# Attention with two versions, swapped: which version an engine jumps over, a group of rows loaded earlier, and a sign set first

## The reference

```python
x = x + xattn(ctx_1024, layernorm(x), mask, ...)      # keys and values: 77 rows of context and the 1024 tokens themselves
x = x + ffn(layernorm(x), ...)                        # a shared expert, and 8 routed ones of which each token takes 2

# xattn, per batch
q = ln @ Wq;  k, v = split(concat([xn @ Wkv, ln @ Wkv], axis=1))
sim = einsum(rmsnorm(q) * scale, rmsnorm(k));  attn = softmax(where(mask, sim, -max))
out = (attn @ v).reshape(b, m, h * d) @ Wout + bout
```

## Time and profile before

| | |
|---|---|
| median of 3 runs | 2512.72 us (2511.25 to 2514.61) |
| the profiled execution's own time | 2512.38 us |
| its span | 2510.8 us |
| TensorE busy | 2415.3 us, 96% |
| VectorE busy | 1754.5 us, 70% |
| ScalarE busy | 1689.5 us, 67% |
| GpSimd busy | 1203.4 us, 48% |
| mean granted TensorE clock | 0.985 |

### The profile page before, as it was taken

One profiled execution on the slowest core, in us unless ns is written; L12 is line 12 of the kernel. 1 busy time (PEld: TensorE's weight loads), 2 busy tenths in 40 slices (PEclk: granted clock), 3 DMA queues, 4 the chain that ended last, 5 costly groups with the idle time before them and its releaser, 6 DMA issues. The chain is left out here.

```text
span 2510.8 us, 53736 instructions
## 1 busy us (share of the span) xinstructions
PE 2415.3 (96%) x19926; PEld 2009.8 (80%) x19926; DVE 1754.5 (70%) x2452; ACT 1689.5 (67%) x2286; POOL 1203.4 (48%) x783
## 2 busy tenths in 40 slices
PE   4899999999999999999999999988989999999997
PEld 3677777777777777777777777658989999999997
DVE  7666766676667676766676667666875559777775
ACT  2588888888888888888888888872333345454443
POOL 5434533453445344534453444415515527777766
PEclk9799999999999999999999999998989999999999
DMA  6323232323332323233333232247804279999996
GB/s 198 148 79 119 92 99 91 127 83 100 98 118 92 102 87 127 85 103 94 117 97 102 86 123 91 66 123 168 200 10 142 89 238 317 322 327 316 320 326 166
DMA packets 231532, 363.25 MB, mean 145 GB/s; under 512 B 59559, under 2 KB 139739, under 8 KB 227400
## 3 DMA queue, kind: packets, MB, share of 16 engines
q1 hardware_dynamic: 204694, 301.66, 39.0%
q0 software_dynamic: 25696, 58.82, 8.1%
q10 hardware_dynamic: 978, 0.34, 0.1%
HBM read 280.90 MB, written 79.85 MB: 144 GB/s over the span
## 5 line engine op out<-in xcount | busy, mean ns | idle before, releaser
L730 DVE TENSOR_TENSOR pr_lo<-ps_s,pr_hi 128x1024 fp32r<-128x1024 f32 x448 | 547.1, 1221 | 310.3 <-ACT ps_s L838 310.3
L837 ACT ACTIVATE pr_hi<-ps_s 128x1024 fp32r<-128x1024 f32 x512 | 526.6, 1029 | 135.6 <-PE ps_s L985 118.3
L472 POOL TENSOR_TENSOR rs<-ss,minus_half 128x16 f32<-128x16 f32 (+1 forms) x96 | 225.8, 2352 | 556.1 <-DVE ss L705 556.1
L1694 ACT ACTIVATE ht<-f_ps_h,b 128x256 f32<-128x256 f32 x440 | 184.4, 471 | 338.3 <-PE f_ps_h L1626 285.4
L838 ACT ACTIVATE ps_s<-ps_s 128x1024 f32<-128x1024 f32 x384 | 395.5, 1030 | 0.0
L1021 PE MATMUL ps_o<-pr_hi,vA 64*65 64x512 f32 x1780 | 380.5, 391 | 0.0
L1021 PE MATMUL ps_o<-pr_lo,vA 64*65 64x512 f32 x1780 | 380.1, 390 | 0.0
L1021 PE MATMUL ps_o<-pr_hi,vC 64*65 64x512 f32 x1780 | 379.6, 390 | 0.0
L1626 PE MATMUL f_ps_h<-xT_hi,w 128*128 128x256 f32 x1760 | 355.2, 285 | 2.5 <-DVE xT_lo L1728 2.3
L951 PE MATMUL ps_m<-w_sb,lnT_sb 64*128 64x384 f32 (+1 forms) x3072 | 329.2, 337 | 11.5 <-POOL w_sb L528 4.8
L1639 PE MATMUL f_ps_y<-w,h_hi 128*128 128x256 f32 x1760 | 326.1, 283 | 0.0
(11 more groups left out here) (219 smaller groups left out, 4716.0 us busy)
## 6 DMA issues: line engine op xcount, KB each, us to landing
w<-w1S_dram SPq DMA_DIRECT2D x160, 512.0 KB, 7.2
lnT_sb<-lnT_dram SPq DMA_DIRECT2D x31, 2304.0 KB, 8.7
w2raw<-in_L_ffn_Wproj SPq DMA_DIRECT2D x78, 512.0 KB, 7.1
w1S_dram<-cut POOLq DMA_DIRECT2D x36, 512.0 KB, 3.0
rec<-rden_dram SPq DMA_DIRECT2D x63, 256.0 KB, 3.7
routed_dram<-empty POOLq DMA_DIRECT2D x28, 387.0 KB, 3.4
xt<-routed_dram SPq DMA_DIRECT2D x39, 258.0 KB
w_raw<-in_L_xattn_Wkv SPq DMA_DIRECT2D x66, 128.0 KB, 2.9
```

What stands on the lines that cost most here:

```text
L472: g.tensor_tensor(rs[:, 0:sums], ss[:, 0:sums], minus_half[:, 0:sums], ALU.pow).then_inc(s_pool, 1)
L730: v.tensor_tensor(pr_lo[:, ring(w, d), :], full_of(d), pr_hi[:, ring(w, d), :].bitcast(F32), ALU.subtract).then_inc(s_lo, 1)
L837: act.activation(pr_hi[:, ring(w, d), :], ps_s[:, d % 2, :], ACT.Exp, bias=bias)
L1694: ins = act.activation(ht[:, p, i, :], ps_h[:, p % 2, i, :], ACT.Gelu_apprx_tanh, bias=b1[:, slot, p, i:i + 1])
```

## The change

Four things are done.

`either` asks the opposite question, so the general body stands first and the bounded one second: with flag 1 an engine now jumps at the start, over the general body, and goes straight on at the end.

VectorE runs the two windows of the opening before it calls `either`; they are the same in both versions. The other engines call it where they did.

SyncE loads the rows of group 2 in attention too, behind those of group 1, once `a[0]` has been split (`c_lo` at 4). It no longer waits at the end of attention for the landing of group 1; ScalarE waits for the two landings (`s_rows`) in `project_out`.

GpSimd sets its sign `s_lop` as the first thing in `project_out`, and SyncE's two signs by hand are gone.

```diff
@@ class Carry
+        self.s_rows = [t.sem("c_rows1"), t.sem("c_rows2")]
@@ attention
         def either(eng, body):
             eng.wait_ge(s_bound, 4)
-            with eng.If(eng.value_load(bounded[0:1, 0:1], min_val=0, max_val=1) > 0):
+            with eng.If(eng.value_load(bounded[0:1, 0:1], min_val=0, max_val=1) < 1):
+                body(True)
+            with eng.Else():
                 body(False)
-            with eng.Else():
-                body(True)
@@ SyncE, last window
                     sp.wait_ge(c_lo, 2)
-                    carry.load_a(sp, attT, 0, 1, c_a1)
+                    carry.load_a(sp, attT, 0, 1, carry.s_rows[0])
+                    sp.wait_ge(c_lo, 4)
+                    carry.load_a(sp, attT, 0, 2, carry.s_rows[1])
@@ SyncE, end of attention
-            sp.wait_ge(c_a1, 32)
@@ VectorE
             def dve_windows(general):
-                windows(dve, window)
-                after = Window(WINDOWS // 2, 0)
-                output(after, 1, 1)
+                for s in range(2):
+                    window(Window(0, s), general)
+                with dve.Fori(1, WINDOWS // 2 - 1) as v:
+                    for s in range(2):
+                        window(Window(v, s), general)
+                for s in range(2):
+                    window(Window(WINDOWS // 2 - 1, s), general)
+                output(Window(WINDOWS // 2, 0), 1, 1)
+            for s in range(2):
+                window(Window(-1, s), False)
             either(dve, dve_windows)
@@ project_out, SyncE
-                    if b == 0 and q < 2:
-                        sp.sem_inc(s_a[q], 32)
-                    else:
+                    if b > 0 or q > 2:
                         carry.load_a(sp, attT, b, q, s_a[q])
@@ project_out, GpSimd
         def _(pool):
+            pool.sem_inc(s_lop, 1)
             pool.dma_start(bo[:, :], ...).then_inc(s_bo, 16)
...
             pool.wait_ge(s_half, 1)
             pool.wait_ge(s_bo, 16)
...
-            pool.sem_inc(s_lop, 1)
@@ project_out, ScalarE
-                    act.wait_ge(s_a[q], b * 32 + 32)
+                    if b > 0 or q > 2:
+                        act.wait_ge(s_a[q], (b + (q > 2)) * 32)
+                    elif q > 0:
+                        act.wait_ge(carry.s_rows[q - 1], 32)
```

More of the change, by code:

```diff
@@ L231, in attention @@
         s_den, s_inv, s_put, s_rec, s_norm = (t.sem("a_" + n) for n in ("den", "inv", "put", "rec", "norm"))
-        c_wo, c_a0, c_a1, c_hi, c_lo = (t.sem("c_" + n) for n in ("wo", "a0", "a1", "hi", "lo"))
+        c_wo, c_a0, c_hi, c_lo = (t.sem("c_" + n) for n in ("wo", "a0", "hi", "lo"))
         s_zero, s_clear = t.sem("a_zero"), t.sem("a_clear")
@@ L715, in lower @@
                     v.tensor_tensor(carry.a_lo[0][n - 3], carry.a[0][:, h, :], carry.a_hi[0][n - 3].bitcast(F32), ALU.subtract).then_inc(c_lo, 1)
-            def dve_windows(general):
[L718 to L753, removed]
-                windows(dve, window)
-                after = Window(WINDOWS // 2, 0)
-                output(after, 1, 1)
@@ new lines, in window @@
+            def window(w, general):
+                for d in range(UNITS):
+                    if w.first and d == 0:
+                        dve.wait_ge(p_lnT, 128)
+                    if w.attend:
+                        if general and d % KT == 0:
+                            maximum(w, d // KT)
+                        if d == 1 and not w.first:
+                            output(w, 1, 1)
+                        if d == KT + 1:
+                            output(w, 0, 0)
+                        dve.wait_ge(s_exp, w.n(UNITS, d + 1))
+                        v.tensor_tensor(pr_lo[:, ring(w, d), :], full_of(d), pr_hi[:, ring(w, d), :].bitcast(F32),
+                                        ALU.subtract).then_inc(s_lo, 1)
+                    if w.attend and not w.first:
+                        if d == 5:
+                            invert(w, 1, 1)
+                        if d in (7, 12):
+                            divide(w, (d - 7) // 5, 1)
+                    if w.attend and d == 13:
+                        invert(w, 0, 0)
+                    if closing(w) and w.s == 1 and d == 16:
+                        divide(w, 0, 0)
+                    if w.turn:
+                        for i in TURNED.get(d, ()):
+                            turned(w, i)
+                    if w.turn and d in (3, 5):
+                        values(w, d == 5)
+                    if w.proj and d in (12, 17):
+                        squares(w, (d - 12) // 5)
+                    if closing(w) and w.s == 1 and d in (4, 6, 9, 11):
+                        lower(d)
+                    if d == 2 and not (isinstance(w.v, int) and (w.v == -1 or 2 * w.v + w.s == WINDOWS - 1)):
+                        squares(w, 2 - GROUPS)
+                    if isinstance(w.v, int) and w.v == -1:
+                        opening(w, d)
```

## The result

The changed kernel takes 2516.84 us (median of 10 runs, 2513.25 to 2520.95), the kernel before 2510.87 us (10 runs, 2507.56 to 2514.61): ratio 1.0025, 95% interval 1.0017 to 1.0033. It is slower by 6.0 us. I had forecast +6.0 us and 2518.6; the absolute time is lower mainly because the kernel before is itself 1.5 us faster over ten runs than in the execution that my sum started from. The profiled execution of the changed kernel took 2516.33 us (span 2514.8), that of before 2512.38 (2510.8).

A forecast was written before the change was run, and what follows sets the result against it. Attention was taken as bound by TensorE, so delays before or early in it are not made up. Terms 2.4 + 7.3 - 3.7 = +6.0 us on 2512.4 gave 2518.6 us; range 2506 to 2524.

The forecast's parts named there:

- The price of a taken branch: Far jump between the two versions: 2.5 us with quiet DMA engines, 5.4 to 6.9 us with busy ones.
- term B: VectorE's jump between opening and attention: TensorE's first product with the values 5.2 us later, plus 2.1 us low clock; +7.3 us.
- the second rival: Pages come at the quiet price, loads still queue at the end: 2510.2 us, no difference; chance 0.17.
- Term A: Jump at the start on TensorE, ScalarE, SyncE, GpSimd: TensorE's 5.4 us fetch delays the opening; +2.4 us passed on.
- Term C: End of attention: no far jump, earlier barrier and first product group, but x queues behind the third rows; -3.7 us.
- The third rival: Start costs as forecast, but x does not wait behind the third rows: 2512.3 us, no difference; chance 0.15.
- the signs that I had named: Times to check in the profile, among them GpSimd's first power 49.6, VectorE's branch near 104, first low part near 110.
- The fourth rival: TensorE's page at the start waits until the opening burst ends at 36 us: term A 6.0, 2522.2 us; chance 0.03.
- the fifth: A short branch remains at the bounded version's end; if it costs a fetch, barrier as late as now, about 2518.6 us.

The follow-up runs named there:

- dve_quiet: Changed kernel with VectorE's branch moved ahead of the fifth step of its second opening window, at 71.7 us, DMA nearly quiet; 2510.16 us, ratio 0.9998.
- swap_alone: Changed kernel with loads and GpSimd's sign as before, keeping the swapped versions, VectorE's opening outside and SyncE's wait left out; 2517.08 us, ratio 1.0030.
- rows_sign_alone: Kernel before, versions in old order, with third group's rows loaded in attention, GpSimd's sign first and SyncE's wait left out; 2507.88 us, ratio 0.9992.

## Why the prediction was right

**The price of a taken branch** held, and was tested at places that the kernel before does not have. Of one engine, VectorE: 2.8 us at DMA share 0.03, 5.2 at 1.03, 5.8 at 0.64 (32.7 to 38.5 us), 7.2 at 1.04 (100.5 to 107.65), and at the end of attention 6.9 before and 8.5 with more in flight. ScalarE's 2.5 and TensorE's 4.6 to 5.7 us fit. At the place of term B four kernels have it, with 5.7 (share 0.89), 6.7, 7.2 and 7.5 us (1.04 in these three). It is not a smooth function of the share, but quiet and loaded are a factor of two to three apart. That settles the second rival: the rule of the Trainium skill, "DMA: Bandwidth & Descriptors", section "Queues, rings and completion order", from which I had it that a page would hardly wait for data, does not describe what was measured: the page's packet started 5.3 us after the branch under load and 1.0 us after it without. The rule of the Trainium skill, "Runtime: NRT & Kernel Launch", section "Instruction fetch mechanics", does: dve_quiet's 2.8 us is a far fetch with almost nothing beside it.

**Term A (+2.4 us)** fits in size, but is not visible in the two profiles. In the changed kernel GpSimd's first power was 1.4 us later, and the first scores 0.4 us earlier (94.67 against 95.10), because the block of 23 projections ahead of them ran at full clock by luck of where the chip's clock stood:

```profile
92.26 2.73 PE L960 MATMUL ps_m<-w_sb,lnT_sb 64*128 64x384 f32 x23 [0.36 <-ACT raw L791]
```

In the profile of before it took 4.38 us, at 0.50. GpSimd's first power, ahead of that block, is a steadier mark: 46.8 to 47.2 us in the six kernels whose TensorE does not jump at the start, 48.3 to 48.6 in five that jump with VectorE's opening outside (50.3 in swap_alone), so 1.5 us. At the scores of several kernels the term looks larger: with TensorE in the old order the scores are at 106.6, 106.1, 103.4, 104.0 and 103.8 us (mean 104.8), with it jumping at the start and VectorE's wait gone at 107.2 and 107.9: 2.8 us, with 3 us of scatter in the first group. So 1.5 to 2.8 us is what the profiles give.

**Term B (+7.3 us)** was right: from 107.2 and 107.9 to the changed kernel's 114.3 are 6.4 to 7.1 us, and the medians of dve_quiet and the changed kernel differ by 6.7. Of its two parts the wait was 5.4 us (109.02 against 103.61; forecast 5.2) and the low clock 2.3 (forecast 2.1). The wait came out that close by two errors that cancel: the fetch took 7.2 us instead of 6.2, and the branch stood at 100.5 instead of 101.3, since the opening was not late there.

**Term C (-3.7 us)** was too small: x2 came 4.8 us sooner behind the last matmul (24.3 instead of 29.1), the stage as a whole 5.1. Its path was the one in the trace: the barrier 2.0 us behind the last matmul's start (forecast 1.9), the first product group almost 10 us sooner behind that matmul (2.3 instead of 12.0), third rows, x and low half in the order that I gave, and the second group behind the low half, from a low clock. The size was off because x was there 9.9 us behind the barrier where I had 11.5. What I had not seen is what swap_alone shows: without the early rows and the early sign the end gains the same 4.8 us, by VectorE's path, so those two parts of the change are worth nothing here and the term is the jump's. I had not said either that the barrier can only come that early because SyncE's wait for the second group's rows is gone.

The third rival (x does not wait behind the third rows, so that the gain at the end pays for the start) falls: GpSimd waited for x until 9.9 us behind the barrier, and 6.9 us (for the bias) without the third rows. No arrangement of the loads that ran brought x2 below 24 us.

**The sum.** 2.8 + 6.7 - 5.1 = +4.4 us; the medians differ by 6.0 (the interval is 4.3 to 8.3). The 1.3 us that the experts' stage took longer in the profile (687.8 against 686.5 us from the last matmul of the output projection) may be part of it, but over all kernels that stretch varies from 684.4 to 687.9 without a pattern, so it is not explained. That the medians give the forecast +6.0 us is in part luck. In the pair of profiles attention's last matmul comes 7.8 us later, where terms A and B gave 9.7, and the stage behind it is 5.1 us shorter instead of 3.7; the executions differ by 4.0 us. Of the signs that I had named, GpSimd's first power (49.6, measured 48.6), VectorE's branch (104, measured 100.5) and its first low part (110, measured 107.7) came earlier than forecast. The fourth rival (TensorE's page waits for the end of the burst) falls with the branch's 5.08 us (its price should also read 2522.0 us by its own terms, 6.0 + 7.3 - 3.7, not 2522.2), the fifth with the barrier.

## What to carry to other kernels

Two long bodies behind one branch cost a far jump on every engine, at one end or the other. Which end is free differs by engine: place each engine's jump where that engine has slack and, above all, where the DMA engines are quiet. Do not let an engine take it between two stages in which another waits for its first result, since there it costs the fetch and then the low clock. An earlier start of a stage can be worth nothing where its second step then waits for another input: here x, in the changed kernel. And an engine's wait that costs nothing today, as SyncE's for the rows, can be the next limit once a jump ahead of it is gone.

## What the runs showed of the hardware

A 4 KB store of ScalarE's took 1.3 us when the third rows had landed (rows_sign_alone: issued 1699.72, the load behind it 1701.05), 3.9 us without the third rows in flight (swap_alone) and 6.9 us behind them (1699.76 to 1706.65 above). Its size says nothing of its price there.

The same kernel before ran between 2508.3 and 2515.7 us on one chip (27 executions). The opening, with TensorE at 1.2 GHz in some gaps and 2.4 in others, carries about 3 us of such differences: 103.4 to 106.6 us for the same scores in kernels with the same opening on TensorE, 111.1 to 114.9 in those with the changed kernel's. Two profiles alone cannot tell a term of 2 us in that stretch.
